# One full-array product for the first 128 tokens of each w unit, and a reordered last chunk

## The reference, cut to what matters

```python
A_bar = exp(dt[..., None] * A)                 # (b, t, d, n)
B_bar = (A_bar - 1) / (A + 1e-8) * x[..., None] * B_t[:, :, None, :]
h = A_bar[t] * h + B_bar[t]                    # for t = 0..2047
y[t] = einsum("bdn,bn->bd", h, C_t[t])
x = x + y + D_skip * x
e = argmax(softmax(layernorm(x) @ Wr.T + br))  # one expert for each token
x = x + gelu(layernorm(x) @ W1[e] + b1[e]) @ W2[e] + b2[e]
```

## Time and profile before

| what | us |
|---|---|
| median of 3 runs | 726.18 (724.6 to 726.65) |
| the profiled execution | 726.01, span 724.3 |
| scan phase (first to last scan) | 20.0 to 445.1 |
| expert phase | 445.1 to 724.3 |

### The profile page before, as it was taken

The page is one execution under the profiler, slowest core; times in us unless marked ns, Lnnn a source line. Parts: engine busy times, 40 slices in busy tenths (PEclk is TensorE's granted clock), DMA queues, the critical chain, the costliest instruction groups (busy, mean ns, idle before and its releaser), DMA issues.

```text
span 724.3 us, 17510 instructions
## 1 busy us (share of the span) xinstructions
PE 682.5 (94%) x5826; PEld 574.6 (79%) x5827; DVE 538.0 (74%) x950; ACT 482.6 (67%) x1005; POOL 485.6 (67%) x616
## 2 busy tenths in 40 slices
PE   8899799999999998899998989999999999999997
PEld 7777677777787776678776778898999999977776
DVE  7799889989989989999999878887343333344441
ACT  3887999998998997899998586433232323233451
POOL 3889998998998987989989587233343434343331
PEclk9699999999999999999999799999999999999999
DMA  6787542342343243143242077711111111111010
GB/s 235 269 258 254 204 145 78 104 148 93 108 152 117 82 137 107 60 148 117 83 125 88 30 256 240 277 41 49 58 52 59 48 58 45 58 38 33 25 45 16
DMA packets 42290, 82.21 MB, mean 114 GB/s; under 512 B 4824, under 2 KB 12637, under 8 KB 42208
## 3 DMA queue, kind: packets, MB, share of 16 engines
q1 hardware_dynamic: 37600, 68.58, 28.7%
q0 software_dynamic: 4608, 12.59, 5.4%
HBM read 69.35 MB, written 13.37 MB: 114 GB/s over the span
## 4 chain that ended last, share of the span: by engine, by line
PE 58%; ACT 12%; POOL 9%; issue 7%; DVE 2%; DMA 1%; SPq 0%; POOLq 0%; ACTq 0%; DVEq 0%
PE WW L1172 16%; PE misc L1209 15%; PE WW L1055 10%; POOL w_sb L667 7%; PE YY L1093 7%; ACT w_sb L835 5%; ACT Csb L825 5%; PE misc L1204 2%; PE WW L1166 2%; DMA w_sb<-c_rows 1%; PE YY L1141 1%; PE misc L969 1%; ACT xin L805 1%; PE misc L981 1%; DVE w_sb L1336 1%
## 5 line engine op out<-in xcount | busy, mean ns | idle before, releaser
L667 POOL TENSOR_TENSOR w_sb<-w_sb,Csb 128x512 f32<-128x512 f32 x224 | 282.7, 1275 | 41.9 <-DVE w_sb L1336 37.7
L1055 PE MATMUL WW<-b_sb,xin 64*128 64x130 f32 (+2 forms) x2304 | 203.3, 293 | 23.4 <-DVE w_sb L1336 12.5
L1055 PEld LDWEIGHTS WW<-b_sb,xin 64*128 64x128 f32 x2304 | 168.4, 192 | 70.3 <-issue 30.6
L1336 DVE TENSOR_TENSOR_SCAN w_sb<-WW,hlast,w_sb 128x512 f32<-128x512 f32 x170 | 210.1, 1269 | 13.5 <-issue 6.5
L835 ACT ACTIVATE w_sb<-dt,negA 128x512 f32<-128x512 f32 x256 | 169.5, 709 | 4.0 <-DVE w_sb L1336 2.0
L916 ACT ACTIVATE dt<-WW,b1c 128x128 f32<-128x128 f32 x256 | 72.8, 387 | 129.2 <-PE WW L1172 129.0
L1093 PE MATMUL YY<-sm,w_sb 128*128 128x128 f32 x1024 | 142.4, 284 | 6.2 <-DVE row L1384 4.3
L729 POOL DMA_INDIRECT y_out<-CbX,ocol x36 | 42.6, 1184 | 142.0 <-DVE CbX L1758 137.3
L1093 PEld LDWEIGHTS YY<-sm,w_sb 128*128 128x128 f32 x1024 | 113.4, 143 | 21.2 <-issue 4.3
L825 ACT ACTIVATE Csb<-w_sb,invA 128x512 f32<-128x512 f32 x150 | 102.5, 713 | 23.2 <-POOL w_sb L667 21.5
L1209 PE MATMUL misc<-w_sb,dt 128*128 x512 | 115.7, 379 | 0.5 <-issue 0.5
(11 more groups left out here) (304 smaller groups left out, 817.7 us busy)
## 6 DMA issues: line engine op xcount, KB each, us to landing
w_sb<-c_rows SPq DMA_DIRECT2D x86, 256.0 KB, 3.3
CbX<-c_rows SPq DMA_DIRECT2D x42, 256.0 KB, 3.3
w_sb<-w_in SPq DMA_DIRECT2D x20, 512.0 KB, 5.7
token_rows<-row SPq DMA_DIRECT2D x8, 1024.0 KB, 4.6
w_sb<-w_in SPq DMA_DIRECT2D x24, 256.0 KB
xin<-x_in SPq DMA_DIRECT2D x8, 512.0 KB, 3.8
w_sb<-x_in SPq DMA_DIRECT2D x7, 512.0 KB, 7.9
b_sb<-b_in SPq DMA_DIRECT2D x1, 780.0 KB, 8.3
```

Of the source, the lines that this page charges most:

```text
L667: eng.tensor_tensor(hc[g % NHC], hb_of(g), Csb[i % NCS][:, :], ALU.mult).then_inc(s_hcp, 1)
L1055: return eng.matmul(to[:, a:a + width], x_rows[rows, k, h * P:(h + 1) * P], band[rows, k, at:at + width], start=start, stop=not start, ski ...
L1336: eng.tensor_tensor_scan(hb_of(g) if pooled(g) else w_of(g), w_of(g), A[g % NA], hlast[(q - 1) % 2][:, h * N + n:h * N + n + 1] if q % NC ...
```

## The change

- Tile 0's two half products become one product with all 128 rows, 129 tokens wide (258 columns), from a second, wider band. It runs behind the first phase and ahead of the second, which has three half products left. The order within the phases changes.
- POOL makes both bands for each pair: 258 and 3 x 130 = 390 elements instead of 520.
- `VECTOR_UNITS` has 21 units instead of 16: chunks 1, 2, 3, 5 and 6 get one more each.
- In the last chunk the early lists come ahead of u: `early1` in units 3 and 4, on the other PSUM bank, u in units 6 and 7, the rest of the hops one unit later; `first_table` runs one step after each of the first five scans; the three weight loads are issued one by one in units 11 to 13; gathers, `keep_ids` and u times x move as shown.
- The small constants grow by 129 columns; the part of b2 that is loaded at the end of the scan phase grows from 1560 to 1944 columns, since the bands lie there.
- `place_tokens` gets one step less, and is cut into other parts; two small tiles move into constants that are no longer used.

```diff
-VECTOR_UNITS = [(4, 8, 12)] + [(5, 12)] * 4 + [(8,)] * 2 + [(4, 10, 15)]
+VECTOR_UNITS = [(4, 8, 12)] + [(4, 8, 12)] * 3 + [(5, 12)] + [(4, 12)] * 2 + [(6, 11, 15)]
...
-        at = {1: [("cbt", q)], 3: [("u_a", q)], 4: [("u01", q), ("u23", q)], 6: [("early1_a", q)], 7: [("early1", q)],
-              8: [("xnr0", q - 1)], 9: [("xnr1", q - 1)], 10: [("routeT", q - 1)], 11: [("route", q - 1)],
-              13: [("turn", 0)]}
+        at = {1: [("cbt", q)], 3: [("early1_a", q)], 4: [("early1", q)], 6: [("u_a", q)], 7: [("u01", q), ("u23", q)],
+              9: [("xnr0", q - 1)], 10: [("xnr1", q - 1)], 11: [("routeT", q - 1)], 12: [("route", q - 1)],
+              14: [("turn", 0)]}
...
-                    if q == NQ - 1 and n == 9:
+                    if q == NQ - 1 and n in (11, 12, 13):
                         eng.wait_ge(s_full, HOP["early1", q] + 1)
-                        for i in range(17, 20):
-                            load_weights(i)
+                        load_weights(n + 6)
...
+                eng.tensor_tensor(wide_bands[pair % NR].rearrange("p (t s) -> p t s", s=2),
+                                  col("wide_band").unsqueeze(2).to_broadcast([P, P + 1, 2]),
+                                  brow[q % B][:, 0, N + 2 * p:N + 2 * p + 2].unsqueeze(1).to_broadcast([P, P + 1, 2]), ALU.mult)
                 eng.tensor_tensor(bands[pair % NR].rearrange("p i (t s) -> p i t s", s=2),
-                                  col("band").unsqueeze(1).unsqueeze(3).to_broadcast([P, TI, HALF + 1, 2]),
...
+                                  col("band").unsqueeze(1).unsqueeze(3).to_broadcast([P, TI - 1, HALF + 1, 2]),
...
-                    if last and n in (9, 11, 13):
+                    if last and n in (8, 10, 12):
...
-                    product(0, 0, start=True)
                     product(1, 2, start=True)
-                    product(0, 1)
+                    product(0, 1, start=True)
                     product(1, 3, width=2 * HALF)
                     product(1, 1, at=2 * HALF, width=2).then_inc(s_wf, 1)
+                    eng.matmul(to[:, 0:WIDE], x_rows[:, 0, h * P:(h + 1) * P], wide_bands[pair % NR], start=False, stop=True,
+                               skip_group_check=True)
                 else:
                     eng.wait_ge(s_wf, m + 1)
                     product(0, 2)
-                    product(1, 0)
-                    product(0, 3)
-                    product(1, 1, width=2 * HALF).then_inc(s_wv, 2)
+                    product(1, 1, width=2 * HALF)
+                    product(0, 3).then_inc(s_wv, 2)
...
-                    if (j, gap) in (((9, 1), (11, 1)) if last else ((30, 0), (31, 0))):
-                        u_times_x(q, int(j in (11, 31)))
+                    if (j, gap) in (((15, 1), (16, 1)) if last else ((30, 0), (31, 0))):
+                        u_times_x(q, int(j in (16, 31)))
...
-                    if last and 0 <= 2 * j + gap - 2 <= 4:
-                        first_table(2 * j + gap - 2)
-                    if last and (j, gap) == (17, 0):
+                    if last and gap and j <= 4:
+                        first_table(j)
+                    if last and (j, gap) == (11, 0):
                         keep_ids()
```

More of the change, by code:

```diff
@@ L40 @@
 BAND = 2 * (HALF + 1)
+WIDE = 2 * (P + 1)
+BANDS = WIDE + (TI - 1) * BAND
 NR, NA, NH, NHC, NCS, NW, NB = 3, 4, 8, 8, 3, 4, 6
@@ L56 @@
 EPS = 1e-5
-SMALL = dict(ident=P, logA=KD * N, wr=KD * CS, umask=1, wcd=KD * CBD, wdt2=D, skip=D, band=HALF + 1, last=1,
+SMALL = dict(ident=P, logA=KD * N, wr=KD * CS, umask=1, wcd=KD * CBD, wdt2=D, skip=D, band=HALF + 1, wide_band=P + 1, last=1,
              b1=E * KH, tri=P, br_row=1, e_less8=E, e_base=E, tok0=NT, j128=32, tile_no=ENTRIES - SURE, turned=2 * len(SPLIT))
@@ L72 @@
 SOON = 4
-ODD = ("u01", "xn0", "bcd", "dt2_0", "dt2_1", "rank", "spread", "early0", "early1")
+ODD = ("u01", "xn0", "bcd", "dt2_0", "dt2_1", "rank", "spread", "early0")
 PARTS = ("bcd_a", "u_a", "early0_a", "early1_a")
@@ L241, in build @@
         ring_at = (E // 4) * KH * D
-        band_at = NR * TI * BAND
+        band_at = NR * BANDS
         def ring(i):
@@ L266, in build @@
         Csb = [Csbs[:, i * TC:(i + 1) * TC] for i in range(NCS)]
-        bands = [b2_sb[:, i * TI * BAND:(i + 1) * TI * BAND].rearrange("p (i t) -> p i t", t=BAND) for i in range(NR)]
+        wide_bands = [b2_sb[:, i * BANDS:i * BANDS + WIDE] for i in range(NR)]
+        bands = [b2_sb[:, i * BANDS + WIDE:(i + 1) * BANDS].rearrange("p (i t) -> p i t", t=BAND) for i in range(NR)]
         brow = [sb(f"brow{b}", [P, TI, 2 * N])[:, :, :] for b in range(B)]
@@ L347, in build @@
         ids = sb("ids", [P, FAR_B + 1], U32)
-        most = max(b - a for a, b in BATCHES) * TI
         listed = row[:, 0, 0:E * CAP]
@@ L351, in build @@
         counted = sb("counted", [P, (E + 1) * CAP], BF16)
-        where = sb("where", [P, 3, most])
-        lane = sb("lane", [P, 1])
+        where = col("logA").rearrange("p (a k) -> p a k", a=2)
+        lane = col("tri", 33, 34)
         spare = sm[:, OFF["wcd"][0]:OFF["skip"][1]]
@@ L690, in emit @@
                         rstd(1, q)
-                    if last and n in (9, 11, 13):
-                        t = (9, 11, 13).index(n)
+                    if last and n in (8, 10, 12):
+                        t = (8, 10, 12).index(n)
                         gather(t, t, 0)
@@ L863, in emit @@
                         copy_first_W1()
-                    if not first and n == (13 if last else 14):
+                    if not first and n == 14:
                         softmax_exp(q - 1)
@@ L1055, in product @@
                     return eng.matmul(to[:, a:a + width], x_rows[rows, k, h * P:(h + 1) * P],
-                                      band[rows, k, at:at + width], start=start, stop=not start, skip_group_check=True)
+                                      band[rows, k - 1, at:at + width], start=start, stop=not start, skip_group_check=True)
                 if part == 0:
@@ L1428, in choose, with place_tokens @@
                     eng.tensor_tensor(onehot[:, 0:tiles, :], over_e(top), less8, ALU.is_equal).then_inc(s_oh, 1)
-            def place_tokens(batch, parts=(0, 1)):
+            def place_tokens(batch, parts=(0, 1, 2)):
                 q0, q1 = BATCHES[batch]
@@ L1444, in place_tokens @@
                     done(eng.tensor_copy(totals[:, :, 0:1], before), "rt")
+                if 1 in parts:
+                    keep = z[1][:, 256:256 + E * (tiles + 1)]
                     done(eng.tensor_tensor_scan(runs[batch], keep,
                                                 ranks[:, 128:128 + (tiles + 1) * E], 0.0, ALU.mult, ALU.add), "rt")
-                if 1 not in parts:
+                    done(eng.tensor_tensor(slot, slot, run[batch][:, :, 0:tiles].rearrange("p e i -> p i e"), ALU.add), "rt")
+                if 2 not in parts:
                     return
-                done(eng.tensor_tensor(slot, slot, run[batch][:, :, 0:tiles].rearrange("p e i -> p i e"), ALU.add), "rt")
                 done(eng.tensor_tensor(slot, slot, onehot[:, 0:tiles, :], ALU.mult), "rt")
                 done(eng.tensor_reduce(slotf, slot, AX.X, ALU.add), "rt")
-                row_at, column, sum_at = (where[:, i, 0:tiles] for i in range(3))
-                done(eng.tensor_scalar(sum_at, slotf, 1.0 / P, -(P - 1) / (2.0 * P), ALU.mult, ALU.add), "rt")
-                done(eng.tensor_scalar(column, sum_at, ROUND, None, ALU.add), "rt")
+                row_at, column = (where[:, i, 0:tiles] for i in range(2))
+                done(eng.tensor_scalar(column, slotf, 1.0 / P, -(P - 1) / (2.0 * P), ALU.mult, ALU.add), "rt")
+                done(eng.tensor_scalar(column, column, ROUND, None, ALU.add), "rt")
                 done(eng.tensor_scalar(column, column, ROUND, None, ALU.subtract), "rt")
@@ L1557, in between @@
                             aggregate(1, q - 1)
-                        if (j, gap) == ((24, 0) if last else (26, 0)):
+                        if (j, gap) == (26, 0):
                             logits(q - 1)
@@ L1566, in between @@
                     if q == BATCHES[0][1] + 1 and j == 2:
-                        place_tokens(0, (gap,))
+                        place_tokens(0, (1, 2) if gap else (0,))
                     if q in (NQ - 3, NQ - 2) and gap and j in range(10, 26, 2):
@@ L1571, in between @@
                         keep_half()
-                    if last and 0 <= 2 * j + gap - 2 <= 4:
-                        first_table(2 * j + gap - 2)
-                    if last and (j, gap) == (17, 0):
+                    if last and gap and j <= 4:
+                        first_table(j)
+                    if last and (j, gap) == (11, 0):
                         keep_ids()
-                    if last and (j, gap) == (28, 1):
+                    if last and (j, gap) == (30, 0):
                         eng.wait_ge(s_full, HOP["turn", 0] + 1)
@@ L1824 @@
     band[one, one % HALF + 1] = -1.0
```

(5 more changed lines are left out.)

4 lines of the change are left out of this document (2 added, 2 removed).

## The result

The changed kernel takes **767.31 us** (median of 4 runs, 767.25 to 769.65), the kernel before 726.4 beside it: a ratio of 1.0561 [1.0522, 1.0599], slower. The profiled execution took 767.25, 41.2 more than before, with a span of 765.4. First the page: the busy time of each engine, and the chain that ended last by engine, in the changed kernel and, last, in the kernel before.

A forecast was written before the change was run, and what follows sets the result against it. PE was taken as the bound. Growth of 6.5 us in chunk 0, 35.6 in chunks 1 to 6 and 1.1 in the last, 43.2 in all, on 726.01 gave 769 us, range 750 to 782 (8 in 10: 745 to 784).

The forecast's parts named there:

- The unit: w's unit on PE: 0.43 us for columns, 0.20 twice for shape changes, less 0.32 for the filled wait: 0.51 more.
- 0.2 later than within a shape: On PE, the wide product's weight load was to start 0.2 us later than one between products of the same shape.
- The other signs: Chunks 1 to 6 at 56 to 60 us, PE free 1 to 2, w's records 2.1 a unit, DVE waiting for w.
- Removal on PE worth nothing: In w's two phases, dropping tile 0's half products shortens neither, since the other row group sets the time: 0 us.
- How much shows: Over the chunks, PE's free time absorbs part of 8.2 us each: chunk 0 grows 6.5, chunks 1 to 6 35.6.
- POOL, DVE and ACT at no cost: In the scan phase, POOL's bands (3.4 us a chunk) and DVE's added units cost nothing while PE is the bound.
- The last chunk: Chunk 7 grows by 8.2 us of PE work less 4.6 absorbed and 2.5 of clock gain: +1.1 us.
- my 2.5 us: Credit in the last chunk for half of the up to 5 us that PE's half clock costs there.
- mended by the order: In the last chunk, early lists and single loads remove SP's 19.8 us stall and C's late rows (8.79 us).
- The rival in which the last chunk makes the kernel faster: Last chunk falls from 57.5 to about 51 us and w's growth is absorbed: 720 us, chance 0.04.
- POOL as the bound: Rival: in the scan phase POOL's bands decide, not PE: +15 less about 5 in the last chunk, 736 us; chance 0.05.
- A free change of shape: Rival: shape changes inside w's unit cost nothing, so it grows 0.12 us, up to 0.25: 722 to 731; chance 0.07.

The follow-up runs named there:

- w on half the array: Kernel before with only the new w and bands, tile 0's wide product cut to rows 64 to 127 and 256 columns: 733.34 us.
- two columns: The run with w on half the array, plus one product per unit on all 128 rows but two columns wide: 807.16 us.

## Why the prediction was right

It said 769 us, and 767.31 came, by the mechanism named: PE is the bound, and w's unit grows across two changes of the array's shape. Step by step:

**The unit: 0.51 forecast, 0.50 measured.** Its parts are less exact than the sum. From the wide product's load to the second phase's, 0.43 of streaming and 0.20 for the change back were forecast, and 0.64 measured. Ahead of the wide product I took 0.32 off for the wait on s_wf and put 0.20 on for the change, net -0.12. Measured from load to load, the part shrank from 0.89 (the first phase in the kernel before: a unit's 1.53 less 0.64 for the second) to 0.75, net -0.14. The half product, which needs no change of shape and shows no idle time before its load, tells the two apart: 0.66. So the wait cost 0.22 to 0.23 and the change behind the two short columns 0.09. Both were about 0.1 too large, and they stand against each other. The sign to look for, "0.2 later than within a shape", was right for the change back and too large for this one. That 0.51 met 0.50 is therefore in part luck.

**The other signs.** The stretches forecast for chunks 1 to 6 were 56 to 60 us, with 1 to 2 free on PE; they are 57.3 to 60.2, with 0.0 to 2.7 free. w's matmul records take 2.10 us a unit, 2.1 forecast. DVE's idle time before scans is put down to PE's line of w, as said.

**Removal on PE worth nothing.** Right: with the wide product ahead of both phases, these take 1.53 us from the first load to YY's, the same as before the change with two half products more.

**How much shows.** 128 x 0.50 is 64 us of PE; the free time fell by 33.9 - 12.3 = 21.6. The chunks, forecast and measured: 6.5 and 2.4; 3.8 and 4.9; 6.8 and 6.7; 6.9 and 6.6; 6.4 and 6.6; 4.0 and 6.2; 7.7 and 7.0; 1.1 and 0.5. Sums: 43.2 and 40.9. Five of eight lie within 0.7. Chunk 0 came out 4.1 under the forecast and chunk 5 2.2 over it, which in part cancel, so the sum is nearer than its parts by luck. In chunk 5, 1.7 of it is clock: 6.83 us at half clock, against 58.56 without any where the product was alone, and 58.48 without any in the run without wide bands, which has the same units on DVE. In chunk 0 the mean clock rose from 0.88 to 0.91, worth about 1.4 by estimate (0.12 of 54.87 less 0.09 of 57.31), and PE found 1.1 us more to absorb than I had let it (2.7 left instead of 3.8); the remaining 1.6 I can't name.

**POOL, DVE and ACT at no cost.** Right for this kernel, on the two grounds tested: without the wide bands nothing changed, and without DVE's five units and the new last chunk the time is the same within its interval. The bands took 0.615 and 0.840 us (forecast 0.64 and 0.85). What I left without a price is what DVE's units cost when PE's cover is gone: 8 us, not nothing. And w on half the array, without the five units and with PE's unit at 1.53 again, was still 7.6 us (1.3%) above the kernel before. In chunks 2 to 4, at full clock in both, it was 1.1, 0.7 and 0.6. POOL's bands could do that (0.39 a pair, 3.2 a chunk before anything absorbs it; forecast 0.9 to 3.4), but some of the 7.6 is clock (34 us at half clock instead of 27), and no run took the bands away from that kernel, so it stays a reading.

**The last chunk.** The size was right (+1.1 forecast, +0.5 measured), the cause given was not. Early lists and single loads took away the stall and C's late rows, as said:

```profile
SPq L536 <- PE misc L1024: 1.8, 1, 1.8
```

Alone that gave nothing (58.15 for 57.51). What came back is clock, and more of it than my 2.5 us: 10.25 us at half clock became 3.41, worth up to 3.4. It did not come with the new order, which alone left 10.24, while the product alone had the old order and no half clock in this chunk at all. Over the runs the length of this chunk goes with its time at half clock and not with its order. With the new w it is 55.98 (old order) and 56.49 (new order, wide product first) without any half clock, and 57.99 (new order) with 3.41:

```profile
432.55:489.04 56.49, 52.99 (x441) 42.94 (x440) 49.44 (x70) 41.24 (x66) 46.93 (x53) 1.00 0.49 154
```

With PE's unit at 1.53 it is 57.51 (old order) and 58.15 (new order) with 10.2, and 55.20 (old order, w on half the array) and 55.66 (new order, DVE's five units) with 6.8. So the step "mended by the order" failed, and the credit stood for another reason: that the sum for this chunk came out is luck. What shortened the stretch at half clock is open. The rival in which the last chunk makes the kernel faster falls with it.

**The rivals.** POOL as the bound: refuted by the run without wide bands. A free change of shape: refuted by the loads of the unit, and by two columns that cost 0.72 us, some 0.5 of it at the changes of shape. The rule of the Trainium skill's "TensorEngine Tiling (Array Packing)", Key Properties, that a change of tiling mode drains the engine, agrees with the 0.20 and the 0.63 of these rows; so does its other one, that different tiles, here the two row groups, run in parallel, with the 0.22 of the half product. What no run took apart is a kernel with the whole product at an unchanged shape, since rows 0 to 63 and 64 to 127 would then write the same columns side by side.

## What to carry to other kernels

Before you replace half-array products by one full-array product, look at what stands on either side of it: the price is its own columns, plus some 0.1 to 0.2 us at each border (a change of the array's shape), plus all that the row groups did side by side there. A product may look free in a semaphore wait (here 0.22 us) and still cost twice that. And read the gain of a repair off the chunk alone, not off the chain: a stall taken out of the last chunk's chain gave nothing, and the chunk's length went with PE's clock instead.

## What the runs showed that was not expected

- The two columns on the full array cost more (unit 2.25 us) than 258 columns in one product (2.03), because they came on top of the half product's two passes and did not replace them.
- The stretches at half clock move with edits that do not touch PE's work there. In the changed kernel there are three in the scan phase; the window of the last:

```profile
441.01:444.42 3.41, 2.88 (x14) 2.91 (x15) 3.41 (x6) 2.28 (x4) 3.41 (x4) 0.50 0.20 68
```

They are the 1.2 GHz level; the three are 10.24, 6.83 and 3.41 us long. How busy PE was ahead of such a stretch does not tell when one comes. In the last chunk it was busy for 9.16 of 12.13 us with the new order alone (10.24 at half clock followed), for 11.79 of 12.81 in the changed kernel (3.41 followed), and for 12.90 of 13.01 with the two columns, where 23.89 followed. With the new w alone it was busy for 11.08 of 12.00 in the same place, and the clock stayed full. The last two as windows:

```profile
458.20:471.21 13.01, 12.90 (x105) 10.40 (x103) 12.42 (x26) 8.90 (x15) 10.60 (x11) 1.00 0.21 65
...
425.00:437.00 12.00, 11.08 (x89) 8.77 (x87) 11.41 (x24) 7.89 (x13) 10.20 (x10) 1.00 0.19 55
```

The mean clock also differs between executions of one kernel: with the product alone it was 0.984 to 0.993, for 770.24 to 762.54 us, and the execution profiled is the one at 0.993. So what decides it is open, and what is read here from one profile's clock holds for that execution.
